# Projection and MoE 0's dispatch in one block, the first group of tiles dispatched before the rest is projected

## The reference, cut to what matters

```python
x = x + w_proj @ attention(layernorm_c(x))          # layer 0, first half
t = to_tokens(x)
n = layernorm(t)                                    # over the 256 features, eps 1e-5
logits = n @ router_w.T                             # 8 experts
rw, re = top_k(softmax(logits), 2); rw /= rw.sum()  # two experts for each token
out = n
for e in range(8):
    out += combine[:, e] * (gelu(n @ w1[e] + b1[e]) @ w2[e] + b2[e])
t = t + out
```

## Time and profile before

| | us |
|---|---|
| median of 3 runs | 2374.78 (2374.61 to 2377.22) |
| the profiled execution | 2370.15, its span 2368.4 |
| attention's loops end, the projection's first matmul | 1302.18 |
| dispatch block's first instruction | 1334.71 |
| first scatter issued by POOL | 1356.96 |
| last scatter issued by POOL | 1439.62 |
| experts block's first instruction | 1448.03 |

### The profile page before, as it was taken

The page is one execution under the profiler, slowest core; times in us unless marked ns, Lnnn a source line. Parts: engine busy times, 40 slices in busy tenths (PEclk is TensorE's granted clock), DMA queues, the critical chain, the costliest instruction groups (busy, mean ns, idle before and its releaser), DMA issues. The chain is left out here.

```text
span 2368.4 us, 84181 instructions
## 1 busy us (share of the span) xinstructions
PE 1993.9 (84%) x29091; PEld 1535.1 (65%) x29092; DVE 2005.2 (85%) x3574; ACT 1770.3 (75%) x2810; POOL 781.3 (33%) x599
## 2 busy tenths in 40 slices
PE   4749999999999999999998724965897339999995
PEld 2426766666666666666666624862685229999994
DVE  5869999999999999999999763759797738888883
ACT  5669999999999999999998663746687626666662
POOL 5321124133222111222124274540264743333331
PEclk8969999999999999999999757986898569999998
DMA  2013323223223223232233253543124722222225
GB/s 85 1 36 86 84 74 91 77 75 94 72 76 93 72 78 91 73 85 84 74 91 107 60 174 108 152 136 112 39 71 135 223 73 49 48 49 49 45 50 158
DMA packets 296699, 203.17 MB, mean 86 GB/s; under 512 B 153579, under 2 KB 277958, under 8 KB 296358
## 3 DMA queue, kind: packets, MB, share of 16 engines
q1 hardware_dynamic: 276838, 166.33, 25.1%
q0 software_dynamic: 19776, 35.73, 5.7%
HBM read 64.79 MB, written 112.92 MB: 75 GB/s over the span
## 5 line engine op out<-in xcount | busy, mean ns | idle before, releaser
L629 DVE TENSOR_TENSOR plow<-prob 128x1024 f16<-128x1024 f32 (+1 forms) x1024 | 1127.6, 1175 | 1.8 <-ACT prob L536 1.8
L536 ACT ACTIVATE prob<-scores 128x1024 f32<-128x1024 f32 x1024 | 998.9, 1026 | 90.4 <-PE scores L689 61.1
L709 PEld LDWEIGHTS outp<-vs,prob 128*128 128x128 bf16 x7680 | 516.0, 98 | 278.9 <-issue 217.6
L709 PE MATMUL outp<-vs,prob 128*128 (+1 forms) x7680 | 604.4, 194 | 26.0 <-DVE plow L629 13.9
L689 PE MATMUL scores<-qT,kT 128*128 (+1 forms) x2048 | 611.6, 380 | 6.3 <-DMA kT<-shift_rows 1.9
L711 PE MATMUL outp<-vs,plow 128*128 (+1 forms) x7680 | 601.7, 194 | 0.0
L711 PEld LDWEIGHTS outp<-vs,plow 128*128 128x128 f16 x7680 | 503.1, 97 | 59.3 <-issue 0.3
L490 POOL TENSOR_TENSOR osum<-osb 128x128 f32<-128x128 f32 x63 | 231.7, 3678 | 832.3 <-DVE rec L634 832.3
L1615 POOL DMA_INDIRECT token_sums<-m1eyo,m1edest x71 | 133.5, 1881 | 277.5 <-DVE m1eyo L1580 134.3
L1450 PE MATMUL m1eph<-m1exT,m1ew1c 128*128 128x128 f16 x3408 | 203.1, 220 | 0.0
L1450 PEld LDWEIGHTS m1eph<-m1exT,m1ew1c 128*128 128x128 f16 x3408 | 194.2, 98 | 0.5
(11 more groups left out here) (397 smaller groups left out, 3389.5 us busy)
## 6 DMA issues: line engine op xcount, KB each, us to landing
sorted_rows<-zero SPq DMA_DIRECT2D x128, 522.0 KB, 4.6
staged<-qk SPq DMA_DIRECT2D x73, 128.0 KB, 2.4
m0exr<-sorted_rows SPq DMA_DIRECT2D x71, 130.5 KB, 2.3
m1exr<-sorted_rows SPq DMA_DIRECT2D x71, 130.5 KB, 2.4
ls_got<-expert_rows SPq DMA_DIRECT2D x8, 1024.0 KB, 5.5
na_staged<-in_L_ffn_W_dram SPq DMA_DIRECT2D x16, 512.0 KB, 3.2
m1dstg<-in_L_ffn_W_dram SPq DMA_DIRECT2D x16, 512.0 KB, 5.3
tok<-in_x_dram SPq DMA_DIRECT2D x8, 512.0 KB, 9.0
```

The costliest lines, as they stand in the source:

```text
L536: act.activation(prob[g % PBUF][:, :], scores[g % 2][:, :], ACT.Exp, scale=1.0 / (QK_SCALE * QK_SCALE)).then_inc(prob_ready, 1)
L629: dve.tensor_tensor(l[:, 0:n], p[:, 0:n], high(p)[:, 0:n], ALU.subtract).then_inc(low_ready, 1)
L709: pe.matmul(to, high(prob[g % PBUF])[:, cols], v, start=(g == 0 and i == 0 and j == 0), stop=False, skip_group_check=True)
```

## The change

The projection block is gone. A dataclass `Projection` carries its buffers into `dispatch`, which for MoE 0 does both. What each engine does in which order comes from one list, `joined_order()`, of steps ("p", tile) project, ("a", group) aggregate the statistics and take the root, ("b", group) scale factors and first two normalised tiles, ("d", tile) dispatch steps of one tile, ("r", group) route. All engines walk the same list.

```diff
+def joined_order():
+    order = [("p", i) for i in range(G)] + [("a", 0), ("p", G), ("b", 0), ("p", G + 1)]
+    order += [("d", t) for t in range(G)] + [("p", 10), ("r", 0)]
+    order += [("p", i) for i in range(11, 16)] + [("a", 1), ("p", 16), ("b", 1)]
+    p = 17
+    for g in range(1, NGR):
+        for t in range(g * G, (g + 1) * G):
+            order.append(("d", t))
+            if p < NT:
+                order.append(("p", p))
+                p += 1
+                if p % G == 0:
+                    order.append(("a", p // G - 1))
+        if g + 1 < NGR:
+            order.append(("b", g + 1))
+        order.append(("r", g))
+    return order
...
-        stg = [sb(f"stg{u}", [P, WC]) for u in range(3)]
+        stg = proj.room if proj else [sb(f"stg{u}", [P, WC])[:, :] for u in range(3)]
...
+        if proj:
+            pl = [pt[:, E_N:E_N + G * E_N].rearrange("p (t e) -> p t e", e=E_N)] * 2
+            xp = [ps(f"xp{u}", [P, 512]) for u in range(2)]
+            pp = [ps(f"pp{u}", [P, 512]) for u in range(2)]
```

On DVE:

```diff
+            def add_projected(i):
+                dve.wait_ge(x_taken, i + 1)
+                dve.wait_ge(projected, i + 1)
+                dve.scalar_tensor_tensor(out=tok[:, i, :], in0=pp[i % 2][:, 0:D], scalar=1.0 / W_SCALE, in1=tok[:, i, :],
+                                         op0=ALU.mult, op1=ALU.add).then_inc(summed, 1)
+            if proj:
+                split_gate()
+                pending = []
+                for kind, i in joined_order():
+                    if kind == "p":
+                        add_projected(i)
+                    if kind in "pa":
+                        for t in pending:
+                            measure(t)
+                        pending = [i] if kind == "p" else []
+                    if kind == "a":
+                        dve.wait_ge(measured, (i + 1) * G)
+                        aggregate(NORM_PARTS[i])
+                    if kind == "b":
+                        scales(i, NORM_PARTS[i])
+                    if kind == "d":
+                        prepare(i)
+                        if i == G:
+                            first_bias_low()
+                    if kind == "r":
+                        route(i)
+                for i in range(NP):
+                    low(i)
```

On ACT:

```diff
+                    if kind == "d":
+                        if i % G + 2 < G:
+                            normed(i + 2)
+                        take(i)
+                        if i == G - 1:
+                            first_bias_high()
+                        for t in range(2 * (i - NT + G), 2 * (i - NT + G) + 2):
+                            if t >= 0:
+                                add_normed(t)
+                for i in range(NP):
+                    high(i)
+                act.activation(warm[:, :], eps[:, :], ACT.Exp)
+                for t in range(2 * G, NT):
+                    add_normed(t)
```

On PE, behind the wait for the router's split weights (`gate_step`) that stood at the block's start before:

```diff
+            def project(i):
+                if i >= 2:
+                    pe.wait_ge(summed, i - 1)
...
+            if proj:
+                pending = []
+                for kind, i in joined_order():
+                    if kind == "p":
+                        project(i)
+                    if kind == "d":
+                        turn(i)
+                    if kind in "pdr":
+                        for t in pending:
+                            mult(t)
+                        pending = [i] if kind == "d" else []
+                    if kind == "r":
+                        rank(i)
```

More of the change, by code:

```diff
@@ L814, in _ @@
             dve.wait_ge(low_ready, N)
[L817 to L898, removed]
@@ new lines @@
+@dataclass
+class Projection:
+    x_dram: object
+    xg: list
+    ah: object
+    al: object
+    wh: object
+    wl: object
+    room: list
+def joined_order():
[15 more added lines that the diff above has]
+    return order
@@ new lines, in measure @@
+            def measure(i):
+                dve.wait_ge(summed, i + 1)
+                dve.bn_stats(stats[:, i, :], tok[:, i, :]).then_inc(measured, 1)
+            if proj:
+                split_gate()
[19 more added lines that the diff above has]
+                for i in range(NP):
+                    low(i)
+            else:
+                for c in NORM_PARTS:
+                    aggregate(c)
+                scales(0, NORM_PARTS[0])
+                split_gate()
+                scales(1, NORM_PARTS[1])
+                for t in range(NT):
+                    prepare(t)
+                    if t == G and narrow:
+                        first_bias_low()
+                    if t == 1 and not narrow:
+                        dve.wait_ge(b_turned, 1)
+                        dve.tensor_copy(b1t[:, :, :], pb[:, 0:E_N * NF].rearrange("p (e n) -> p e n", n=NF)
+                                        ).then_inc(b_taken, 1)
+                    if t in route_after:
+                        route(route_after[t])
+                    for i in parts_after(t - LAG):
+                        low(i)
@@ L1258, in _ @@
                 if t == G - 1 and narrow:
-                    act.wait_ge(b_in, 16)
-                    act.activation(b1h[:, :], b1n[:, :], ACT.Copy, scale=W_SCALE).then_inc(b_high, 1)
+                    first_bias_high()
                 if t == 2:
@@ L1272, in _ @@
                 act.activation(b2t, b2t, ACT.Copy, scale=W_SCALE)
-            if add_norm:
+            if add_norm and not proj:
                 for t in range(NT - G, NT):
@@ L1328, in _ @@
         def _(pool):
+            if proj:
+                for q in range(1, AQ):
+                    if q > 1:
+                        pool.wait_ge(ah_ready, q - 1)
+                    pool.tensor_tensor(quarter(proj.al, q), quarter(tok, q), quarter(proj.ah, q), ALU.subtract
+                                       ).then_inc(al_ready, 1)
             if narrow:
```

200 lines of the change are left out of this document (129 added, 71 removed).

## The result

The changed kernel takes 2398.76 us, median of 4 runs (2393.41 to 2401.92), against 2374.70 (2373.95 to 2377.22) of the kernel before, run beside it: ratio 1.0097, 95% interval 1.0076 to 1.0118, slower by 24 us. The forecast was 2395.5. The profiled execution took 2401.92 us with a span of 2400.2.

The account below looks back on a forecast made before the run. POOL's scatters bound the stage, through when each group's places come. First scatter 19 us earlier, then waits of about 25 and 15 us: last scatter +20.8 us, 2395.5 on the median's scale of 2374.78; eight-in-ten range 2376 to 2403.

Parts of the forecast that it names:

- The sum: Projection and dispatch stage: last scatter at 1460.4 against 1439.62, +20.8 us, with the 8.4 us to the experts unchanged.
- PE's start: Start of the joined block: PE waits for the router's weights and starts 4.6 us later, at 1306.8.
- The first scatter: First group's dispatch: POOL's first scatter at about 1338, 19 us earlier, with POOL's clearing done by then.
- The period: Second and third group's loops: PE and DVE take turns, 3.98 us a tile at 1.2 GHz, 2.85 at 2.4.
- The clock: PE in the second and third group's loops: 1.2 GHz in both, working 60% of each period.
- half case: PE's clock swings, 2.4 GHz in half of the loops' periods: +12 us, or 2387; chance 0.14.
- the first rival: PE's clock stays at 2.4 GHz in one or both loops; both: +4 us, or 2379, chance 0.11.
- POOL's gaps: POOL waits about 25 us before the second group's scatters, 15 before the third's, none before the last.
- The tail: Experts' weights and normalisations behind the last choice: taken as 0, at most +4.5 us; chance 0.10 together with late start.
- The rival "faster": Loops not serial, period about 2.2 us or less, head start stays: gain 4 to 14 us, 2361 to 2371; chance 0.10.

Follow-up runs that it names:

- joint kernel: Changed kernel; DVE splits the next tile before adding the projected one, router weights after the fourth addition, experts' weights converted one piece per tile: 2366.10 us, ratio 0.9961.
- filled kernel: Changed kernel plus six extra PE matmuls, results unused, behind each projected tile from 17 on: 2382.96 us, ratio 1.0032 to the kernel before.
- skew: Changed kernel with DVE's order alone changed, next tile's split ahead of the projected tile's addition: 2418.53 and 2423.77 us, ratios 1.0071 and 1.0057 to the kernel before.

## Why the prediction was right, step by step

**The sum.** Forecast +20.8 us for the stage, measured +23.2 in the first profile. The median's difference is 24.1. Of the 2.4 us between forecast and profile, 0.6 had gathered when the third group's places came (119.3 us behind the block's start, forecast 118.7). Another 1.7 are POOL's own pace: from there to the last scatter it took 41.2 us for 31 steps, 1.33 each. The forecast used 1.275, though its own rows gave 1.312 on average.

**PE's start.** 1306.99 to 1311.58 is the forecast wait of 4.6 us for the router's weights, now DVE's `m0dgates`. That it came out exactly is in part luck. The weights were used 3.2 us after they were asked for, not 4.0, and the first instruction on them took 0.91 us, not 0.17, since POOL's first subtraction ran beside it until 1311.07:

```profile
1310.20 0.91 DVE L1164 TENSOR_SCALAR m0dgate<-m0dgate 128x16 f32<-128x16 f32 x1 [3.04 <-DMA m0dgate<-in_L_ffn_router_w_dram]
```

**The first scatter.** Forecast 35.8 us behind the block's start, measured 37.4 and 38.1. The forecast's own pieces add up to less than it said, 1322.4 + 8.8 + 0.7 + 4.5 + 0.3 = 1336.7 and not 1338, so the rounding hid a part of the miss. Most of the missing piece is one that the prediction priced at nothing: it let POOL's clearing lie beside other work. It doesn't quite:

```profile
1324.97 1.80 POOL L1430 MEMSET m0w<- 128x2048 f16 x1
```

```profile
1324.82 1.99 DVE L1158 TENSOR_SCALAR m0drstd<-m0drstd 128x8 f32<-128x8 f32 x1
1324.98 1.83 DVE L1159 SCALAR_TENSOR_TENSOR m0dshift<-m0dmv,m0drstd 128x8 f32<-128x8 f32 x1
```

The scale factors of the first group take 1.99 us where 0.17 was normal, and tile 0's normalisation waits for them. That is 1.8 us, where 1.6 and 2.3 are missing by the stated 1338, or 2.9 and 3.6 by the sum of the pieces. In the joint kernel the clearing had ended (1319.48) when the same instruction began (1320.05), and it took 0.17 us. Little of this reaches the end, since the second group's places come only 0.6 us later than forecast.

**The period.** Forecast 3.98 us at 1.2 GHz, measured 3.89, with the same two waits facing each other. Forecast 2.85 at 2.4 GHz, measured 2.85 in the filled kernel, where ACT's copy, which the forecast left out, ended as late as PE's projection.

**The clock.** Forecast 1.2 GHz in both loops, measured 0.50 in both windows, without the swing of the half case. Had it been high, the first rival said, the price would be +4 us; the filled kernel, high in both loops, came to +8 (+4 to +11). Fifteen periods shortened by 1.04 us are 15.6; it gained 15.2.

**POOL's gaps.** Forecast about 25 and 15 us and none ahead of the fourth group; measured 25.9, 15.5, none.

**The tail.** Weights and normalisations were given no price, with +4.5 as the bound. The last of this work, DVE's shares, ends at 1472.82, 3.3 us before the experts' start. Right, but by little: from the last tile's copy at 1440.17 it took 32.6 us, the forecast's upper figure of 32. In the joint kernel, whose scatters end earlier, such a tail would be the bound (estimated from this figure, not run).

**The rival "faster".** It said: with a period of 2.2 us or less the head start stays, and the kernel gains 4 to 14 us. The joint kernel is that case, at 1.7 and 2.1 us a tile and a gain of about 10 us. What kept the changed kernel from it was the order, as the forecast held against this rival, and the joint kernel shows that the head start is worth having once the order is right. How much of its 32 us comes from the skew, and how much from the gate's and the weights' place, isn't shown: skew ran alone only on the slower chips. Nor is it separated how much of the skew's part is the broken turn-taking and how much the higher clock that comes with it.

## What to carry to other kernels

When two chains of work are interleaved tile by tile, write down for each engine what stands behind each wait: if A waits for B's result and B's next step waits for something that stands behind that wait on A, the period is the sum of both, though neither engine is full (PE 55%, DVE 45% from 1357 to 1390). Here one independent step taken ahead of the waiting one, on one engine, undid it. And count an early start as a gain only after asking whether the consumer (here POOL, 20.4 us a group) can be kept fed from then on.

## What the runs showed of the hardware

- Idle time of PE cost twice here: once as idle, once as clock. Six matmuls of no use per tile took the granted clock from 0.50 to 0.90 over 1357 to 1390, and the kernel from 1.0094 to 1.0032. With PE busy 18.13 of those 33 us in the changed kernel, the clock didn't swing but stayed at 0.50.
- A DVE TENSOR_SCALAR or CAST of 8 or 16 elements per partition lasted 0.91, 1.99, 2.55 (joint), 4.06 and 3.98 us where POOL had a MEMSET or a subtraction of 128x2048 running, and 0.17 otherwise. Each of the five ended within 0.1 us of POOL's instruction. The additions from PSUM (`scalar_tensor_tensor`, 0.42) and BATCH_NORM_STATS2 beside the same subtractions kept their times. The Trainium skill, "SBUF — State Buffer", section "SBUF: two separate sides", says that a DVE instruction in a two-port mode and a GpSimd instruction share a port pair under an exclusive lock, which one of them holds for its whole length. The traces agree with the lock; in which mode these instructions ran they don't show. Where a small instruction stands on a critical chain, it pays to look at what POOL does then.
- Chips differ: the kernel before took 2374 to 2376 us in three batches and 2400 and 2405 on two other chips, where engines also started up to 11.6 us after the record that they wait for had ended.
